# A fused attention and MLP layer on one core: a score bank for the third head's transposes, the values product by tiles of tokens, and the order of ScalarE's and VectorE's work

## The reference, cut to what matters

```
# layer 0: attention under a mask, then the MLP
q = (layer_norm(x) @ q_w);  k, v = split(layer_norm(context) @ kv_w)
attn = softmax(where(xa_mask, neg, q @ k.T * scale))
x = x + (attn @ v) @ proj_w + proj_b
x = x + gelu(layer_norm(x) @ fc1_w + fc1_b) @ fc2_w + fc2_b
# layer 1
Q, K, V = x @ Wq, kv @ Wk, kv @ Wv        # per head, times the rows' mask
energy = Q @ K.T
lengths = sum(energy[:, :, 0, :] != 0)
energy = where(cols >= lengths, -inf, energy)   # and cols > row, where causal
out = softmax(energy / sqrt(dk)) @ V
x1 = layernorm(x + mha(x, x, causal));  x2 = layernorm(x1 + mha(x1, context))
x = layernorm(x2 + relu(x2 @ fc1.T + b1) @ fc2.T + b2)
```

## Time and profile before

| | us |
|---|---|
| median of 3 runs | 2731.42 (2729.98 to 2732.57) |
| profiled execution | 2731.34 |
| span of its core, first to last instruction | 2729.6 |

### The profile page before, as it was taken

How to read it: one execution, slowest core, us unless ns; L and a number is a source line. 1 busy time by engine, 2 the same in 40 slices (tenths; PEclk the granted TensorE clock), 3 DMA queues, 4 the chain that set the end, 5 groups by cost and what they waited for, 6 DMA issues and landing times. The chain is left out here.

```text
span 2729.6 us, 68429 instructions
## 1 busy us (share of the span) xinstructions
PE 2661.5 (98%) x24040; PEld 2340.1 (86%) x24040; DVE 1904.2 (70%) x5290; ACT 1554.0 (57%) x4789; POOL 750.3 (27%) x947
## 2 busy tenths in 40 slices
PE   7999999999999999999999999999899999999997
PEld 6888888887888888888889999998798988899886
DVE  6777777776544443444377777777688888888876
ACT  6777777776211111111277777777576676767764
POOL 3433333330000000000013333333333433424343
PEclk8999999999999999999999999999899999999999
DMA  4332333252311211022021111112321222212210
GB/s 153 111 113 93 122 110 109 94 155 74 93 49 44 61 46 46 31 61 85 24 94 46 46 46 46 46 46 78 98 78 61 91 71 69 85 61 92 69 46 24
DMA packets 180502, 202.57 MB, mean 74 GB/s; under 512 B 17616, under 2 KB 107728, under 8 KB 179536
## 3 DMA queue, kind: packets, MB, share of 16 engines
q1 hardware_dynamic: 180432, 201.66, 23.3%
HBM read 137.65 MB, written 63.96 MB: 74 GB/s over the span
## 5 line engine op out<-in xcount | busy, mean ns | idle before, releaser
L2865 ACT ACTIVATE mlp_h<-mlp_f,mlp_b1col 128x512 f32<-128x512 f32 x128 | 88.3, 690 | 524.0 <-PE mlp_f L3069 524.0
L3069 PE MATMUL mlp_f<-mlp_xT_hi,mlp_w 128*128 128x512 f32 x1024 | 335.5, 390 | 0.0
L2970 DVE CAST mlp_hT_hi<-mlp_h 128x512 fp32r<-128x512 f32 x128 | 58.2, 455 | 369.9 <-ACT mlp_h L2865 369.8
L3087 PE MATMUL mlp_acc<-mlp_w,mlp_hT_hi 128*128 128x512 f32 x1024 | 315.3, 389 | 0.5 <-DVE mlp_hT_lo L2972 0.5
L878 ACT ACTIVATE mask_prob<-mask_scores,mask_low 128x256 f32<-128x256 f32 x512 | 236.5, 486 | 102.9 <-DVE mask_low L1420 102.9
L878 ACT ACTIVATE cross_prob<-cross_scores,cross_low 128x256 f32<-128x256 f32 x512 | 236.6, 493 | 64.7 <-DVE cross_low L1414 64.7
L878 ACT ACTIVATE causal_prob<-causal_scores,causal_low 128x128 f32<-128x128 f32 (+1 forms) x512 | 210.1, 434 | 88.2 <-DVE causal_low L1420 88.2
L1420 DVE CUSTOM_DVE_ANT_0 mask_scores<-mask_scores,mask_mask 128x256 f32<-128x256 f32 x512 | 198.6, 459 | 46.7 <-PE mask_scores L2074 37.2
L3069 PEld LDWEIGHTS mlp_f<-mlp_xT_hi,mlp_w 128*128 128x128 f32 x1024 | 192.6, 188 | 40.5 <-issue 0.4
L3087 PEld LDWEIGHTS mlp_acc<-mlp_w,mlp_hT_hi 128*128 128x128 f32 x1024 | 192.0, 188 | 40.8 <-DVE mlp_hT_lo L2972 1.0
L172 PE MATMUL causal_work<-causal_xT_hi,causal_w 128*128 128x256 f32 x1008 | 224.4, 296 | 0.8 <-DVE causal_qk_parts L1379 0.8
(11 more groups left out here) (349 smaller groups left out, 8201.5 us busy)
## 6 DMA issues: line engine op xcount, KB each, us to landing
cross_x_in<-after_attention SPq DMA_DIRECT2D x17, 512.0 KB, 4.1
mask_x_in<-in_x SPq DMA_DIRECT2D x16, 512.0 KB, 4.5
mask_c_in<-in_ctx SPq DMA_DIRECT2D x16, 512.0 KB, 5.3
mask_res<-in_x SPq DMA_DIRECT2D x16, 512.0 KB, 3.6
after_attention<-mask_res SPq DMA_DIRECT2D x16, 512.0 KB, 2.8
mlp_x<-after_attention SPq DMA_DIRECT2D x8, 1024.0 KB, 5.5
mlp_stage<-in_L_xattn_fc_w SPq DMA_DIRECT2D x8, 1024.0 KB, 5.6
after_layer<-mlp_y SPq DMA_DIRECT2D x8, 1024.0 KB, 4.4
```

What stands on the lines that cost most here:

```text
L2865: act.activation(h32[:, m % 2, :], F1[m % 2][:], ACT.Gelu, bias=b1col[:, m:m + 1]).then_inc(s["gelu"], 1)
L2970: dve.tensor_copy(hT[0][:, r, :], h32[:, r, :]).then_inc(s["h_hi"], 1)
L3069: ins = pe.matmul(F1[m % 2][:], W[2 * (m // 4)][:, a, k, m % 4 * P:(m % 4 + 1) * P], xT[p][:, k, :], start=(k == 0 and n == 0), stop=(k == ...
L3087: ins = pe.matmul(ACC[t][:], hT[a][:, m % 2, t * P:(t + 1) * P], W[2 * (m // 4) + 1][:, p, m % 4, :], start=(m == 0 and n == 0), stop=(m = ...
```

## The change

Three things are changed. First, head 2's transposes go to head 2's own scores bank (`probs_bank`), except in the last block of mask attention and the first of cross attention; head 3 keeps `PT` to itself. `turn_probs` of head 3 no longer waits for the copy of head 2, but for the bank to be free of `energies0` (`probs_free`), and `scores` wait for one copy more. Second, the values product is cut by tiles of tokens: `values(b, t)` is 12 matmuls of 512 columns, two of them a row block, and `V_BANK` holds one tile of tokens. `attend` of chunk 0 now needs both tiles, and the copy of tile 0 all attends of the block before. In causal attention the copy of tile 1 moves from ACT to DVE. Third, the hand-written orders are changed: on ACT in all three attentions, on PE in causal and cross attention, and on DVE in the opening and first turn of cross attention.

```diff
-    PT_BANK = (SC[0], SC[1], PT, PT)
+    def shared(b):
+        return isinstance(b, int) and (masked_ctx and b == B - 1 or cross and b == 0)
+    def probs_bank(b, u):
+        h = u % HC
+        return PT if h == 3 or h == 2 and shared(b) else SC[h]
...
         ACT:
+        def values(b, t):
+            act.wait_ge(s["v_ps"], 2 * b + t + 1)
+            if t == 0 and (not isinstance(b, int) or b > 0):
+                act.wait_ge(s["av_done"], KC * b)
+            act.activation(V[:, t], V_BANK[:].rearrange("p (h d) -> p h d", d=DH), ACT.Copy
...
         def mask_turn(b, prev, cur, nxt):
             if cur and prev:
-                for u in (0, 1, 2):
-                    exps(b, u)
+                values(b, 0)
+                exps(b, 0)
+                exps(b, 1)
             if prev:
                 pair_kept(b, -1)
             if cur and prev:
+                exps(b, 2)
                 exps(b, 3)
...
             copy(b, 15)
-            if nxt:
-                values(b + 1, 0)
...
         def causal_turn(b, prev, cur, nxt):
...
                 for u in (4, 5, 6):
                     exps(b, u)
+                if nxt:
+                    copy(b, 4)
                 exps(b, 7)
...
-                qk(b, 3)
                 if not nxt:
+                    qk(b, 3)
                     yield ROOM
                 copy(b, 6)
-            if nxt:
-                turned(b + 1, 0)
...
+                if nxt:
+                    qk(b, 3)
...
                 copy(b, 7)
                 if nxt:
+                    turned(b + 1, 0)
                     turned(b + 1, 1)
...
                 exps(b, 9)
-                if nxt:
-                    values(b, 1)
...
         def cross_turn(b, prev, cur, nxt):
...
+                    copy(b, 4)
+                    exps(b, 7)
+                    copy(b, 5)
+                    copy(b, 6)
+                    qk(b, 3)
             if nxt:
                 turned(b + 1, 0)
+            if cur and prev:
+                copy(b, 7)
+            if nxt:
                 turned(b + 1, 1)
...
                 exps(b, 8)
+                if prev:
+                    values(b, 1)
...
         DVE:
+        def values(b, t):
+            dve.wait_ge(s["v_ps"], 2 * b + t + 1)
+            dve.tensor_copy(V[:, t], V_BANK[:].rearrange("p (h d) -> p h d", d=DH)).then_inc(s["v_ready"], 1)
...
             if prev and nxt:
                 add_z(b)
+            if nxt:
+                values(b, 1)
             qk_lo(b, 3)
...
+            if prev:
+                normed_rows(b)
+            if cur:
                 qk_lo(b, 3)
             if nxt and not prev:
                 turned(b + 1, 0)
                 turned(b + 1, 1)
-            if prev:
-                normed_rows(b)
+                shift_parts()
...
             else:
                 shift_through()
+                matrix_lo(3)
             if cur:
                 minima(b, 3, (2, 3) if prev else range(HC))
             if nxt and not prev:
-                matrix_lo(3)
+                matrix_lo(4, (0, 1))
                 qk_lo(b + 1, 0)
+                matrix_lo(4, (2, 3))
...
                 qk_lo(b + 1, 1)
-            if not prev:
-                matrix_lo(4)
...
             yield OPENING
+            minima(0, 1)
+            yield OPENING
             front(1)
             rows_kept(0)
             rows_seen(1)
-            yield OPENING
-            minima(0, 1)
             yield OPENED
...
         PE:
-        def values(b, h, half, part=None):
-            t = half
-            ins = product(pe, V_BANK[:, t * HALF:(t + 1) * HALF],
-                          lambda k, a: cT[a][:, k, t * P:(t + 1) * P],
-                          lambda k, c: W[2][:, c, k, h * HALF:(h + 1) * HALF], part)
+        def values(b, t, part=None):
+            ins = product(pe, V_BANK[:], lambda k, a: cT[a][:, k, t * P:(t + 1) * P],
+                          lambda k, c: W[2][:, c, k, :], part)
...
-                pe.wait_ge(s["copied"], UNITS * b + HC * c - 2)
+                pe.wait_ge(s["copied"], UNITS * b + HC * c - 1)
...
-            if h == 3:
+            if h == (2 if u >= 0 and shared(b) else 3):
+                probs_free(b, u // HC)
+            if h == 3 and (cross and u < 0 or shared(b)):
                 pe.wait_ge(s["copied"], n - 1)
...
-                if c % 2 == 0:
-                    pe.wait_ge(s["v_ready"], 2 * b + 1 + c // 2)
+                if c == 0:
+                    pe.wait_ge(s["v_ready"], 2 * b + 2)
...
             queries(b, 3)
+            if nxt:
+                keys(b, 3, 0)
             energies0(b, 2)
             turn_probs(b, 4)
-            keys(b, 3, 0)
+            keys(b, 3, 1 if nxt else 0)
             turn_probs(b, 5)
...
             turn_probs(b, 6)
             if nxt:
-                values(b, 1, 1, 1)
+                values(b, 1, 1)
...
             if nxt:
+                keys(b + 1, 1, 0)
                 energies0(b + 1, 0)
             turn_probs(b, 12)
```

91 lines of the change are left out of this document (35 added, 56 removed).

## The result

| | us |
|---|---|
| before, median of 5 runs | 2731.61 (2729.98 to 2732.76) |
| changed, median of 5 runs | 2716.79 (2715.76 to 2720.38) |
| ratio | 0.9948, 95% interval 0.9937 to 0.9958 |
| predicted | 2695 (2683 to 2717) |

The change makes the kernel 14.8 us faster, 0.5%, where 36 were forecast. The profiled execution of the changed kernel (span 2718.6 us) is the longest of its five, 3.6 above the median; differences between the two profiles are therefore read turn by turn and not from the spans.

What follows compares the result with a forecast made beforehand. The prediction took PE's queue, busy 98% of the span, to bound the kernel. Its terms, 9.6 + 4.0 + 7.7 + 7.0 + 2.5 + 5.2 = 36.0 us, took 2731.3 to 2695 us, range 2683 to 2717.

Steps and rivals of the forecast that it cites:

- What bounds the kernel: Whole kernel: it is as long as PE's queue; only fewer or cheaper PE instructions, or smaller holes between them, pay.
- The values product: All three attentions: 12 matmuls of 512 columns replace 24 of 256, saving 0.10 us a product, 9.6 us in all.
- Mask attention: Mask turns: pair_kept earlier on ACT removes PE's 0.33 us wait for the kept pair in 12 turns, 4 us.
- Causal attention: Causal turns: head 2's own bank and the keys' order remove waits, 0.55 us a turn, 14 turns, 7.7 us.
- The keys' order: Causal attention on PE: half a keys product ahead of energies0 hides two waits, 2 x 0.13 us a turn.
- Cross attention: Steady cross turns: bank wait of 0.30 gone and 0.20 from transposes 6 moved, 14 x 0.50 = 7.0 us.
- The first cross turn: First turn of cross attention: four DVE edits, together saving 5.2 us, between 0 and 8.
- (a): Cross opening: minima(0, 1) ahead of front(1) on DVE makes PE's hole 5 us instead of 2.25, costing 2.4.
- (b) to (d): First cross turn, DVE: shift_parts earlier, 0.9 to 1.3; qk_lo(1, 0) inside matrix_lo(4), 0.7; matrix_lo(4) done earlier, 5.8 us.
- The openings and ends: First turns of mask and causal attention and last units: single shared-bank waits gone, 2.5 us, between 1 and 3.5.
- The first: Rival: stalls come back; only the values product and first cross turn pay, 14.8 us, 2717 us; chance 0.16.
- The one on the other side: Rival: DVE's copy of the values slows causal attention, about 2737 us; chance 0.03, and 0.04 that it eats just the gain.

Runs made afterwards that it cites:

- halves: The changed kernel with each values product written as 24 matmuls of 256 columns instead of 12 of 512; 2725.25 us.
- lo_first: The changed kernel with post_lo and minima(b, 2, (2, 3)) ahead of turned(b + 1, 0) on DVE in the steady cross turn; 2698.01 us.
- pool_later: The changed kernel with POOL's residual in the steady cross turn waiting until DVE's turned(b + 1, 0) is done; 2703.49 us.
- rows_first: lo_first with DVE's opening of cross attention as before the change: front, rows_kept and rows_seen ahead of minima(0, 1); 2696.58 us.
- weights_late: lo_first with shift_parts, matrix_lo(3) and matrix_lo(4) on DVE where they stood before the change; 2699.55 us.
- before_lo: The kernel before the change with the one DVE edit of lo_first in the cross turn; 2730.90 us.
- one_bank: The changed kernel with heads 2 and 3 sharing one bank in every block, all orders kept; 2735.24 us.
- keys_late: lo_first plus POOL's query0(0, 2) ahead of masked_context(1), with PE's causal keys products behind energies0 as before the change; 2698.19 us.
- pair_late: lo_first with ACT's pair_kept behind the third head's exponentials again in mask attention; 2703.69 us.
- act_values: lo_first plus POOL's query0(0, 2) ahead of masked_context(1), with causal attention's second values copy on ACT instead of DVE; 2696.22 us.

## Why the prediction was wrong

**What bounds the kernel** was right: PE's queue. The kernel without the collision is at 2698.0, 3 us from the forecast of 2695, with mask and causal attention better than forecast by some 2 us and the openings worse.

**The values product** was right: 9.6 us by the pairs, 8.5 by halves.

**Mask attention** was right in mechanism, and low in size: a turn is 0.59 us shorter in the mean, 0.49 forecast with the product. Undone alone, pair_kept's place costs 0.44, the product 0.18, and the bank, counted at nothing there, 0.17. They add up to more than 0.59; that they partly hide each other is likely but not shown.

**Causal attention** was right in size (0.80 a turn with the product, 0.75 forecast), and half right in cause. The keys' order is worth 0.36 rather than 0.26. The 0.24 us ahead of head 3 were put down to the bank; the bank or ACT's order is enough, and only with both undone does the wait return, at 0.9 and not 0.24.

**Cross attention** is the step that failed: "On DVE normed_rows goes ahead of qk_lo(3), which delays that by 1.0 us against about 1.4 of slack; ACT's qk moves behind three copies. Next in line is energies0(3), by 0.2 us." The gain itself came as forecast in sum: lo_first has a turn of 47.72, 0.71 below before, where 0.70 was counted with the product (how it divides isn't shown; the bank alone is worth 0.76 in this order). But the list of what is next in line was made for instructions that PE waits for directly, on the engines that the diff moves. It left out whom post_turn releases. post_turn now comes behind the scores, POOL's residual starts as early against DVE's queue as to stand ahead of turned(b + 1, 0), and the two share something that both need whole. It cost 1.12 us of waiting and 1.43 against the forecast turn (49.16 against 47.73; the rest of it is turned's place ahead of post_lo, 0.32 in pool_later), 14 times, 20 us. The trace of before had the warning: in its tile view the same instruction takes 0.68 or 1.23, and the prediction passed over that.

**The first cross turn** came out low in the two traces, and its terms were mis-sized: 5.2 forecast; measured 2.2 in the turn itself and 0.9 in the next (whose excess over the steady turn went from 0.95 to 0.02), 3.0 without its share of the product. The order of the opening, (a), was charged with 2.4 and cost 0.7 by the marks (rows_first); the hole was where it was forecast, 4.40 us. (b) to (d) were given 7.6 and are worth 3.5 (weights_late): adding up the idle ahead of three instructions counts time that PE then spends waiting at the next ones.

How much this stretch gained depends on the execution too. In ten of the fifteen traces, those of before and after among them, the granted clock is 0.50 for 3.4 us some 11 us ahead of cross attention's first scores (before: from 1906.3). In the other five, before_lo, lo_first, one_bank, keys_late and weights_late, it is 1.00 there, behind the same idle times of PE (1.16 and 0.99 in before and in before_lo), and the first scores come 1.5 us earlier. The kernel before gets nothing out of that: PE then waits 4.22 us for the exponentials instead of 2.25, and from the scores of causal attention's last block to those of cross attention's second it takes 93.88 (before) and 93.97 (before_lo). The changed kernels take 91.2 to 91.5 with the slow stretch (after, pool_later, pair_late) and 89.6 without (lo_first). So the change is worth 2.4 to 2.7 there in one kind of execution and 4.4 in the other, and the forecast of 5.2 missed by less than the two profiles of before and after make it look.

**The openings and ends**, 2.5 forecast, are not seen: the stretches outside the turns above are 1.6 us longer by the marks. The largest part is mask attention's first turn, 1.45 longer, in which DVE waited 7.33 us for a DMA instead of 4.84. This turn takes 41.6 to 44.6 us in the thirteen kernels that hold the change, and 43.05 and 42.67 in before and before_lo, so 1.45 is within what executions differ by. The wait itself is 5.2 to 7.6 us in the thirteen and 4.5 in before_lo, so a part of it may come from the change; its cause is left open. Causal attention's first turn is 1.0 shorter, and what remains is 1.2 longer together.

**The rivals.** The first gave 2717, the time that was measured, for another reason: stalls that come back in all three attentions. None came back in mask and causal attention; in cross attention one came that was not there before and cost more than was gained. That its number fits is chance; added up as the rival is worded, with the 2.5 of the openings, it would have been 2714. The one on the other side, DVE late by the copy of the values, did not happen (act_values).

## What to carry to other kernels

When an instruction moves, follow what it releases, on every engine, and not only what waits behind it: an engine off the critical path that starts 0.8 us earlier can hold up another one that PE waits for. An instruction whose longest duration is twice its shortest on the same shapes is a collision already in the trace; look what the other engine ran, and whether the change moves either. Idle times ahead of successive instructions of one chain don't add up, and an edit that shows no effect when undone alone may be one of two that do the same thing. A wait can have another length in a second trace of the same code, as the opening's 2.25 and 4.22 here: price a term from more than one.

## What the runs showed of the hardware

A VectorE instruction with two inputs in SBUF (128x512, 0.68 us alone) that overlaps a GpSimd tensor_tensor over 128x512 in SBUF takes 1.22 to 1.79 us (before, after, lo_first): it waits for the end of that instruction, whole. In pool_later, where they don't meet, the 28 instances take 0.68 to 0.75. Two inputs are not needed: the COPY `cross_m` of 128x2, 0.15 us in the changed kernel, takes 1.24 in the kernel before, where it overlaps POOL's product. Instructions of VectorE with an input in PSUM are not held up by the same GpSimd instructions. GpSimd is held up in turn: its two products take 2.96 in the changed kernel, where DVE's instruction comes in between, and 2.54 in lo_first, where none does.

Twelve matmuls of 512 columns (f32 in the rows, a weight load for each) take 2.85 us, 24 of 256 columns 2.95: 0.10 us a pair of groups in the trace, and 8.5 us over 96 pairs in the timed runs.

The granted clock can fall in one execution and not in another behind the same instructions and the same idle times: 0.50 for 3.4 us in before, 1.00 in before_lo, in the opening of cross attention. It moved the first scores by 1.5 us.
